# Score tiles in a ring of six PSUM banks instead of five, and one sum bank for all heads

## The reference

```python
xn = layernorm(x)
q, k, v = (xn @ Wq) * mod, (xn @ Wk) * mod, (xn @ Wv) * mod      # mod = cos(phase) * amplitude
scores = einsum('bhid,bhjd->bhij', q, k) / sqrt(8) * cos(2*pi*(i - j)/S)
w = softmax(scores); w = (w + roll(w, 1, axis=-1)) / sqrt(2)
attention = einsum('bhij,bhjd->bhid', w, v) @ Wo
# eight experts, the two best of each token: silu(a) * g @ w2[e].T, weighted and summed
out = x + attention + experts
```

## Time and profile before

| what | us |
|---|---|
| median of 3 runs | 596.96 (596.77 to 598.1) |
| the profiled execution, first to last instruction | 597.7 |
| TensorE matmul busy | 547.4 (92%) |
| ScalarE busy | 527.5 (88%) |
| VectorE busy | 213.0 (36%) |
| exponentials, 410 instructions on ScalarE | 481.8 |
| weighted values, 3968 matmul instructions | 267.3 |
| scores, 1024 matmuls | 191.6 |

### The profile page before, as it was taken

How to read it: one execution, slowest core, us unless ns; L and a number is a source line. 1 busy time by engine, 2 the same in 40 slices (tenths; PEclk the granted TensorE clock), 3 DMA queues, 4 the chain that set the end, 5 groups by cost and what they waited for, 6 DMA issues and landing times.

```text
span 597.7 us, 19051 instructions
## 1 busy us (share of the span) xinstructions
PE 547.4 (92%) x7948; PEld 256.3 (43%) x7948; DVE 213.0 (36%) x499; ACT 527.5 (88%) x487; POOL 94.5 (16%) x102
## 2 busy tenths in 40 slices
PE   2968996888899999999999999999999999999884
PEld 1442332322454544454454545444454545454333
DVE  6866451210321433434342434334343122221134
ACT  2748989999599999999999999999999999999991
POOL 5200165354000101010100101010100101010000
PEclk9977999899799999999999999999999999999999
DMA  8951043113654333232332333333233313200402
GB/s 220 184 176 72 6 137 109 51 52 73 144 159 125 93 86 88 64 90 84 94 94 84 95 90 87 78 77 86 84 95 94 93 44 94 53 12 7 146 2 73
DMA packets 60890, 53.76 MB, mean 90 GB/s; under 512 B 33244, under 2 KB 50294, under 8 KB 60546
## 3 DMA queue, kind: packets, MB, share of 16 engines
q1 hardware_dynamic: 58082, 47.48, 30.8%
q0 software_dynamic: 2272, 4.72, 2.2%
q10 hardware_dynamic: 448, 0.30, 0.2%
HBM read 38.68 MB, written 13.78 MB: 88 GB/s over the span
## 4 chain that ended last, share of the span: by engine, by line
PE 68%; ACT 13%; issue 12%; DMA 3%; DVE 2%; SPq 1%; POOL 0%; ACTq 0%; DVEq 0%
PE ps L1352 32%; PE ps L1326 21%; ACT big L696 12%; PE ps L1259 7%; PE ps L1269 4%; PE ps L1161 2%; DMA acc<-in_L_attn_x 1%; DMA qk_parts<-store 1%; DVE store L783 1%; DMA store<-in_L_ffn_w 1%; PE ps L1296 1%; PE ps L1146 1%; SPq L447 1%; DMA qa<-shift_rows 0%; DMA slots_x<-attnT,slot 0%
## 5 line engine op out<-in xcount | busy, mean ns | idle before, releaser
L696 ACT ACTIVATE big<-ps 128x1536 f32<-128x1536 f32 (+1 forms) x410 | 481.8, 1236 | 29.6 <-PE ps L1326 24.4
L1352 PE MATMUL ps<-big,vh 128*32 128x256 f32 (+1 forms) x3968 | 267.3, 396 | 0.0
L1326 PE MATMUL ps<-qa,ka 49*128 49x512 f16 x896 | 167.6, 392 | 23.0 <-ACT big L696 12.7
L1352 PEld LDWEIGHTS ps<-big,vh 128*32 128x32 f32 x3968 | 108.9, 110 | 115.0 <-issue 67.0
L1326 PEld LDWEIGHTS ps<-qa,ka 49*128 49x128 f16 x896 | 37.7, 94 | 143.7 <-ACT big L696 100.3
L588 POOL DMA_INDIRECT results<-y,row_of x39 | 37.9, 971 | 270.9 <-DVE y L966 269.5
L1259 PE MATMUL ps<-xgT,store 128*32 128x128 f32 x1716 | 66.5, 276 | 3.0 <-DMA store<-in_L_ffn_w 3.0
L1259 PEld LDWEIGHTS ps<-xgT,store 128*32 128x32 f32 x1716 | 55.1, 112 | 18.7 <-issue 6.2
L1029 DVE TENSOR_REDUCE m<-ps 128x1 f32<-128x512 f32 x64 | 44.1, 690 | 31.2 <-PE ps L1363 31.2
L951 DVE SCALAR_TENSOR_TENSOR cs<-cs,ps 128x384 f32<-128x384 f32 x39 | 21.6, 554 | 91.9 <-ACT cs L688 91.9
L966 DVE TENSOR_SCALAR y<-ps,weight_of 128x128 f32<-128x128 f32 x39 | 13.7, 351 | 99.0 <-PE ps L1269 99.0
(11 more groups left out here) (178 smaller groups left out, 199.3 us busy)
## 6 DMA issues: line engine op xcount, KB each, us to landing
store<-in_L_ffn_w SPq DMA_DIRECT2D x39, 352.0 KB, 3.2
store<-in_L_ffn_w SPq DMA_DIRECT2D x39, 192.0 KB, 3.5
qk_parts<-store SPq DMA_DIRECT2D x8, 512.0 KB
qa<-qk_parts SPq DMA_DIRECT2D x27, 128.0 KB
slots_x<-vh SPq DMA_DIRECT2D x8, 330.0 KB, 8.2
cs<-slots_x SPq DMA_DIRECT2D x80, 32.0 KB, 2.7
store<-results SPq DMA_DIRECT2D x4, 512.0 KB, 5.5
ka<-qk_parts SPq DMA_DIRECT2D x31, 64.0 KB
```

Source lines behind the costliest of these rows:

```text
L696: nc.scalar.activation(probs[:, prob_of(tiles[0]):prob_of(tiles[-1]) + 1, :], ps[:, bank_of(tiles[0]):bank_of(tiles[-1]) + 1, :], ACT.Exp, ...
L1326: ins = nc.tensor.matmul(ps[:, bank_of(n), :], k[at:at + KQ, P * o:P * o + P], q[at:at + KQ, CW * c:CW * c + CW], start=True, stop=True, t ...
L1352: ins = nc.tensor.matmul(ps[32 * c:32 * c + 32, O_BANKS[p % 2], cols], vh[:, p % 2, o + 8 * b, :], probs[:, prob_of(n), cols], start=k == ...
```

## The change

- RING becomes 6: groups of 4 and 2 tiles in banks 0 to 5; 171 rounds, 341 groups. `probs` grows to 18 tiles.
- SIDE_BANK becomes 6. One O_BANK (7) sums every head: the first piece of head p waits for the copy of head p-1. `copy_out(p)` moves to the last piece of its own head.
- A round's pieces are split: up to `3r-2` ("early") go between the scores of the large and the small group, up to `3r-1` ("late") after the small group; a part never crosses the end of a head.
- The jobs go to SIDE_BANK, into rounds 20 to 45, three and two a round in turn: after the large group's scores, after the small group's, and at the end. The two exact heads' operands get storage of their own (`qe_store`) and are loaded from round 17 on.
- Experts begin in round 46 with ROUNDS_A_TILE = 3, so every round has a step until round 163. The shifts of exact heads are loaded at round 48.
- Stations in the new rounds: rank 6, rotations 9 to 12, `order_rest` 12, parts 13 and 14, squares 15 and 16, `square_sums` 17. A rotation (all four in SIDE_BANK) waits for the one before it.

```diff
-LARGE_GROUP, SMALL_GROUP = 3, 2
+LARGE_GROUP, SMALL_GROUP = 4, 2
-SIDE_BANK = 5
+SIDE_BANK = 6
-O_BANKS = (6, 7)
+V_BANKS = (7, 5)
+O_BANK = 7
-FIRST_JOB_HEAD = 4
-JOBS_A_HEAD = 8
-JOB_QUAD = 4
-TOP_EXP_AT = 7
-RANK_AT = 7
-GATES_AT = 8
-SECOND_AT = 22
-EXPERTS_AT = 37
+TOP_EXP_AT = 6
+RANK_AT = 6
+GATES_AT = 7
+LATE_AT = 9
+ORDER_AT = 12
+PARTS_AT = (13, 14)
+SQUARES_AT = (15, 16)
+SECOND_AT = 17
+JOBS_AT = 20
+JOBS_DONE = JOBS_AT + 26
+EXPERTS_AT = JOBS_DONE
-ROUNDS_A_TILE = 4
-LATE_AT = 10
-PARTS_AT = (15, 17)
-SQUARES_AT = (19, 20)
+ROUNDS_A_TILE = 3
-EXACT_AT = 156
+EXACT_AT = JOBS_DONE + 2
+        qe_store = sb("qe", [P, S], F32)
...
+        def jobs_of_round(r):
+            at = r - JOBS_AT
+            if at < 0:
+                return range(0)
+            first = 2 * at + (at + 1) // 2
+            return range(min(first, JOBS), min(first + 2 + (at + 1) % 2, JOBS))
...
+        def up_to(done, wanted):
+            head_ends = (done // (QUADS * HALVES) + 1) * QUADS * HALVES
+            return range(done, max(min(wanted, head_ends), done))
         def rounds():
-            done, j, taken = 0, 0, [0, 0]
+            done = 0
             for r in range(ROUNDS + 1):
...
                 ready = min(RING * r, SCORE_TILES) // NC * HALVES
-                even = (RING * HALVES * r - NC) // NC
-                pieces = range(done, max(ready if r == ROUNDS else min(ready, even), done))
-                done = pieces.stop
-                yield r, jobs, pieces
+                early = up_to(done, min(ready, 3 * r - 2))
+                late = up_to(early.stop, ready if r == ROUNDS else min(ready, 3 * r - 1))
+                done = late.stop
+                yield r, early, late
...
-                if r == EXPERTS_AT:
+                if r == SECOND_AT:
                     sp.wait_ge(rows_ready, 2)
                     sp.wait_ge(order_ready, 2)
+                    sp.wait_ge(scratch_wr, 8 * 16)
...
                 if k == 0 and half == 0:
                     pe.wait_ge(vh_ready, p + 1)
-                    after(pe, o_copied, p - 1)
-                    after(pe, m_reduced, jobs_before(p))
-                    if jobs_before(p) == JOBS:
-                        pe.wait_ge(exact_shift_ready, 1)
+                    after(pe, o_copied, p)
...
-            def max_job(p, j, r, i, c):
+            def max_job(j):
+                h, i, c = job_at(j)
                 if j == 0:
                     pe.wait_ge(exact_ld, EXACT * 8 * 16)
-                pe.wait_ge(o_copied, p)
+                    pe.wait_ge(square_ready, 2)
+                    pe.wait_ge(shift_ready, 2)
                 after(pe, m_reduced, j)
...
-            for r, jobs, pieces in rounds():
-                for job in jobs[:-1]:
-                    max_job(*job)
-                for g in groups_of_round(r):
+            for r, early, late in rounds():
+                jobs = jobs_of_round(r)
+                groups = groups_of_round(r)
+                for g in groups[0:1]:
                     scores(g)
-                    if g == 2 * r:
-                        for job in jobs[-1:]:
-                            max_job(*job)
+                for j in jobs[0:1]:
+                    max_job(j)
+                for u in early:
+                    weighted_values(u)
+                for g in groups[1:2]:
+                    scores(g)
+                for j in jobs[1:2]:
+                    max_job(j)
...
-                for u in pieces:
+                for u in late:
                     weighted_values(u)
...
                 expert_work(r)
+                for j in jobs[2:3]:
+                    max_job(j)
+                if r == JOBS_DONE - 1:
+                    turn_maxima()
```

More of the change, by code:

```diff
@@ L1034, in make_exact_shift, with heads_done @@
                 dve.wait_ge(mxT_ready, 1)
-                nc.vector.tensor_scalar(exact_shift[:], ps[0:EXACT * NT, O_BANKS[(p - 1) % 2], 0:P], -1.0 / SHIFT_STEP, -ABOVE,
+                nc.vector.tensor_scalar(exact_shift[:], ps[0:EXACT * NT, SIDE_BANK, 0:P], -1.0 / SHIFT_STEP, -ABOVE,
                                         ALU.mult, ALU.add).then_inc(exact_shift_ready, 1)
-            for r, jobs, pieces in rounds():
[L1039 to L1048, removed]
+            def heads_done(pieces):
                 for w in quads_in(pieces):
                     p, k = w // QUADS, w % QUADS
-                    if p >= 1 and k == 0:
-                        copy_out(p - 1)
+                    if k == QUADS - 1:
+                        copy_out(p)
                     if p == 1 and k == 2:
@@ L1056, in _ @@
                         normalise(p - 1)
-                    if jobs_before(p) < JOBS and jobs_before(p + 1) == JOBS and k == QUADS - 2:
-                        make_exact_shift(p)
                     if p == H - 1 and k == ADD_AT:
                         add_results()
[L1061 to L1065, removed]
+            for r, early, late in rounds():
+                jobs = jobs_of_round(r)
+                m, step = expert_step(r - 1)
+                if step == 0 and m > 0:
+                    result_out(m - 1)
+                if step == 2 and m < TILES:
+                    take_g(m)
+                for j in jobs[0:1]:
+                    take_max(j)
+                heads_done(early)
                 if step == 1 and m < TILES:
                     take_a(m)
-                if step == 2 and m < TILES:
-                    take_g(m)
+                m, step = expert_step(r)
+                if step == 0 and m < TILES:
+                    rows_out(m)
+                for j in jobs[1:2]:
+                    take_max(j)
+                heads_done(late)
+                for j in jobs[2:3]:
+                    take_max(j)
+                if r == SECOND_AT:
+                    key_weights(1)
+                    mean_squares(1)
+                if r == SECOND_AT + 1:
+                    shifts(1)
+                if r == ORDER_AT:
+                    order_rest()
                 if r == RANK_AT:
@@ L1212, in rank_tokens @@
                 pe.wait_ge(ones_ready, ONES)
[L1213 to L1214 removed]
+                nc.tensor.matmul(ps[:, SIDE_BANK, FP:FP + E], tri[:], tokens[:], start=True, stop=True)
+                nc.tensor.matmul(ps[:, SIDE_BANK, FP + E:FP + 2 * E], ones[:], tokens[:], start=True, stop=True).then_inc(rank_ps, 1)
             pe.wait_ge(wmat_ld, 4 * 16)
```

86 lines of the change are left out of this document (34 added, 52 removed).

## The result

The kernel after takes **605.01 us** (median of 4 runs, 604.04 to 607.37); the kernel before, run beside it, 597.10 us (4 runs, 596.77 to 598.1). The ratio is 1.0125, interval 1.0103 to 1.0147: **slower by 1.25%, 7.9 us**. 597.7 was forecast; 605.01 lies inside the range, on its slow side. The profiled execution of the kernel after was the slowest of its four (607.37 us; granted clock 0.976 in the mean, 0.981 to 0.989 in the others).

The account below looks back on a forecast made before the run. TensorE was taken to bound the expert stage, with both engines nearly full overall. Stage terms, ending with experts to 564.9 us and the end, summed to 598.4, which less 0.7 for the profiled execution gave 597.7; range 590 to 607.

Parts of the forecast that it names:

- ScalarE's pace: Four-bank exponentials of 1.885 us, 1.78 from start to start; a round ScalarE sets takes 2.68 us, 0.447 a tile against 0.450.
- Rounds 0 to 19: Stage before the jobs: 20 x 2.68 us plus routing, squares, table loads, clock and rotations, sum 67.0, from 41.6 to 108.6.
- Rounds 20 to 45: Jobs' stage: two rounds with five jobs take 6.7 us; stage 89.5 us, to 198.1, against 69.7 at ScalarE's pace.
- The links: Rounds 20 to 45: job to job through one bank at least 1.18 us; first to second 1.53, second to first 1.31.
- cost 0, cover 1.5 us: Job 0 at 108.4 us: its operands' loads, to about 107, cost nothing, 1.5 us to spare; beyond that each us counts.
- The expert round: Rounds 46 to 163: TensorE sets 3.06 us a round (3.08 with 24 expert matmuls), 358.8 us in 117 rounds.
- The boundaries of heads: Expert stage, one sum bank: waits for the copy at 8 of 11 head ends, 0.53 us each, 4.2; `take_a` adds 1.1.
- twice VectorE's `take_a` comes behind the copy: Expert stage: at two head ends `take_a` queues behind the copy on VectorE, 1.1 us.
- The end: After the experts: six rounds 16.1 us, last exponential 1.9, matmuls until the copy 1.7, then 13.8 as before; experts' sum hidden.
- The faster one (switches hidden): Rival: array switches hidden or four-tile group cheaper, expert rounds fall to 2.84 us; 572 us, 585 with half; chance 0.18.
- longer links: Rival in rounds 20 to 45: job link longer than 1.18 us; at 1.40, 605 us, 608 with low clock; chance 0.20.
- the late operands: Rival at job 0: exact operands land late and TensorE stands; 5 us late gives 603, 10 us gives 608; chance 0.08.

## Why the prediction was right or wrong

The forecast was of no difference, and the kernel is slower by 7.9 us. The mechanisms that it named are the ones that the runs show; what it had wrong is the size of several terms, and two that it put at nothing, job 0's operands and the clock in the jobs' stage. Its sum fell 7.1 us short of the profile (598.4 against 605.5). By its own steps:

- **ScalarE's pace.** Right. Four banks 1.881 us, 1.774 from start to start (1.885 and 1.78 predicted); a round that ScalarE sets 2.66 to 2.68 (2.68). The estimate from the formula in the Trainium skill ("ScalarE: Activation LUTs", What ACT_TABLE_LOAD costs) was 1.892; the trace agrees within 0.6%.
- **Rounds 0 to 19.** Tile 120 at 107.74 instead of 108.6: 0.9 better. The rotation rounds took 3.36 to 3.44 (3.41).
- **Rounds 20 to 45: mis-sized by 4.2 us** (93.7 instead of 89.5). The links were right to 0.02 (1.16, 1.17, 1.54, 1.55). Two rounds were 6.74 instead of 6.69, 0.6 in all. What failed is "cost 0, cover 1.5 us" for job 0: its operands were late. Here are TensorE at job 0 and SyncE's last load.

```profile
107.01 0.60 PE L1338 MATMUL ps<-qa,ka 49*128 49x512 f16 x4 [0.19 <-ACT big L697]
108.98 0.39 PE L1372 MATMUL ps<-ka,qe 49*128 49x512 f16 x1 [1.37 <-DMA ka<-qk_parts]
...
107.08 0.37 SPq L389 DMA_DIRECT2D ka<-qk_parts  x1
```

  The last load was issued at 107.08, as I had it ("16 loads to about 107"), but it has to land too. These loads took 1.9 to 2.2 us from issue to landing, which the cover of 1.5 left out; job 0 started at 108.98, and it could have from 107.6 on. Round 20 took 4.82 us instead of 3.36, so 1.5 of the 4.2. By these times 0.9 of it is what rounds 0 to 19 had won: with the predicted start the wait would have been that much shorter. I had this as a rival at 5 to 10 us with a chance of 0.08. Then come rounds 33 and 34, 5.08 and 3.67 us, with the first weighted values of a head at 1.2 GHz. Here are TensorE's row and the window around it, and then the same row, behind the same wait of 0.30, in the kernel with the split in the job rounds only, where the clock stayed full:

```profile
156.41 1.90 PE L1359 MATMUL ps<-big,vh 128*32 128x512 f32 x8 [0.30 <-DVE osb L1012]
...
155.00:160.00 5.00, 4.70 (x30) 0.90 (x30) 2.11 (x4) 2.71 (x3) 0.32 (x1) 0.66 0.12 30
...
159.72 1.06 PE L1359 MATMUL ps<-big,vh 128*32 128x512 f32 x8 [0.30 <-DVE osb L1012]
```

  There the two rounds take 3.81 and 3.35 us. So the clock cost 1.6 us here, in a stage whose sum had no term for it. The other 0.6 are the copies, `normalise` and round 45, 3.1 us where 2.5 were counted.

- **The expert round: mis-sized by 0.025 us.** 3.08 to 3.09 instead of 3.06 and 3.08, 2.2 us in 117 rounds. Four changes of 0.10 each was nearly the right price. That changing the tiling mode drains TensorE, as the Trainium skill says ("TensorEngine Tiling (Array Packing)", Key Properties), fits the split's cost in two kernels; that it is a drain, and not the first weight loads of the new form, no run here separates.
- **The boundaries of heads.** 6.2 us instead of 5.3. One of them on TensorE and VectorE, round 54:

```profile
226.85 0.39 PE L1338 MATMUL ps<-qa,ka 49*128 49x512 f16 x2
228.28 0.86 PE L1271 MATMUL ps<-xgT,store 128*32 128x128 f32 x22 [1.04 <-DVE cs L952]
...
226.98 0.69 DVE L1012 COPY osb<-ps 128x512 f32<-128x512 f32 x1 [4.26 <-PE ps L1359]
227.59 0.54 DVE L952 SCALAR_TENSOR_TENSOR cs<-cs,ps 128x384 f32<-128x384 f32 x1
```

  VectorE's copy starts at 226.98, `take_a` behind it at 227.59, and the expert step waits 1.04 for that. This was the step "twice VectorE's `take_a` comes behind the copy", and it was right: the two such places, rounds 54 and 150, cost 1.1 each (3.76 + 3.51 instead of 2 x 3.085), and 0.53 + 0.55 had been counted. What was mis-sized are the six other boundaries without cover, 0.65 to 0.71 instead of 0.53 each. In round 65 it is 0.84 us from the start of VectorE's copy to TensorE's next weighted values (261.58 to 262.42), where 0.74 was counted.
- **The end.** 34.1 us from tile 984 instead of 33.5. The copy came at 590.55, 15.0 before the end (13.8 before), with 1.2 GHz granted from 593.4 to 596.8 and again from 603.6. The experts' sum (582.37 to 587.28) was hidden, as predicted.

Together: -0.9 + 4.2 + 2.2 + 0.9 + 0.6 = 7.0. None of the rivals came as it stood. The faster one (switches hidden) is refuted by the same switches in two kernels; longer links did not come (1.17, not 1.40); the late operands came small. The loss lies in the two stages where the forecast put the costs, and no term was far off: small ones, nearly all to the slow side, in stages without slack, which hand each lateness on. That four of the five parts missed to the same side is what carried the sum 7 us away from "no difference".

What stays open: why the low clock came in round 33. It came at a head's end at which TensorE waited 0.30, but the same wait in the kernel with the split in the job rounds only did not bring it, so that wait alone isn't the cause. In the kernel before a like stretch was at 150.8 to 157.7, so it isn't the change's alone either; and since the profiled execution was the slowest of four, the others may have had less of it.

## What to carry to other kernels

Larger groups on one full engine only pay if they take nothing from the full engine beside it. Here ScalarE lost 10.5 us of work, and TensorE got 8.9 more, because each change between two kinds of matmuls costs about 0.10 us and a stage of 118 rounds hands on every one; with the split in the job rounds only, TensorE's busy time is 538.1 us, less than the 547.4 before. Put a fine interleaving only where it covers a wait (the jobs) and leave it out where the engine is full; and space the steps of a chain through one buffer wider than its link (1.17 us here), which brought the same 64 jobs from 0.28 to 0.10 us each over ScalarE's pace. When a large rearrangement gives a small number, read it by stages: here gains and losses of 4 to 8 us stood beside each other.

## What was unexpected of the hardware

- **More waiting came with a lower clock, and with more than the wait's own cost.** With the link lengthened by 0.60 us the granted clock fell from 0.98 to 0.73 in the stage, and the stage lost 44.9 us instead of about 28 (one run). With the waits taken away (two jobs a round) it was 1.00 from 108.0 to 184.1. In the kernel with the split in the job rounds only, TensorE waited 2.06 us for job 0 until 109.94, and 1.2 GHz was granted from 111.5 to 118.4. Not every wait does it, as round 33 shows.
- **A change between scores and weighted values costs about 0.10 us in either direction, nearly the same in three kernels**, and it doesn't show as idle time: the profile counts it as TensorE busy (363.8 us in the expert stage of the kernel after, 348.1 with the split confined to the job rounds, for the same 6104 instructions).
- **Of two long VectorE instructions in a row the second adds 0.60 us, not its 0.69** (maximum and copy both).
